# Indices of all edge blocks loaded once into SBUF, and the gather loop of a graph kernel written out

## The chip, the core and the metric

The kernel runs on one core of one Trainium2 chip. The metric is device time in microseconds of one execution, the median of several runs. The engines by their names in the rows: PE is the tensor engine, DVE the vector engine, ACT the scalar engine, POOL is GpSimd, SP the engine that here only issues DMAs. SPq and ACTq stand for the queues of DMAs issued by these engines.

## The reference

A graph attention network with two layers over 6250 nodes and 106,250 edges, and behind it a mixture of 8 experts. The edges are sorted by their destination.

```python
def _transformer_conv(x, edge_index, Wq, bq, Wk, bk, Wv, bv, Ws, bs):
    q = (x @ Wq.T + bq).reshape(N, H, C)          # H, C = 4, 16
    k = (x @ Wk.T + bk).reshape(N, H, C)
    v = (x @ Wv.T + bv).reshape(N, H, C)
    logits = (q[dst] * k[src]).sum(-1) * (1.0 / np.sqrt(C).astype(np.float32))
    m = jax.ops.segment_max(logits, dst, num_segments=N)
    e = jnp.exp(logits - m[dst])
    denom = jax.ops.segment_sum(e, dst, num_segments=N)
    alpha = e / (denom[dst] + 1e-16)
    msg = v[src] * alpha[..., None]
    out = jax.ops.segment_sum(msg, dst, num_segments=N).reshape(N, HC)
    return out + x @ Ws.T + bs
...
x = x + _L0_gnn_ref(_layernorm(x, axis=-1), edge_index, ...)
x = x + _L0_ffn_ref(_layernorm(x, axis=-1)[None], ...)[0]
```

The part that this document is about is `k[src]` and `v[src]`: for each edge, one row of keys and values is fetched by an index.

## The kernel before

There are five phases with a barrier of all engines between each two. The **setup** normalises the nodes, projects them to q, k, v and a skip path, stores a table of keys and values (`kv_t`, 512 bytes a node) in memory, finds for each node where its edges begin, fills a table with zeros (16 fills, L242) and scatters q to the places where a node's edges start (POOL, L126). The **edge phase** runs twice, once a layer (`edge_phase(0)`, `edge_phase(1)`), with a node phase between them that makes the tables of the second layer. The **expert phase** ends the kernel.

An edge phase works on 104 blocks (`BLOCKS`) of two streams of 512 edges, in 26 steps of four blocks (`UNROLL`). Each engine has its own program, and semaphores set the order:

- SP (L511 to L528) loads for block b, once the block four earlier has been transposed (`kq_turned`) and its logits used (`gaps_ready`): the indices `ix` (L518), the q rows `qz` (L519) and two masks (L521). Its DMAs stand in one queue in this order.
- POOL (L531 to L544) waits for the indices of the block and for its buffer (`v_turned`), and issues 8 gathers (L542) of 128 rows of keys and values each. `gathering` is a semaphore that it counts up and that no engine waits for.
- PE transposes k and q when the gathers have landed (L553, L554), multiplies for the logits (L560), transposes v (L566) and the results (L575 to L577), in four stages that lie one block apart.
- DVE runs the scans over the edges in three stages: held q (L603), the running maximum (L617) and differences (L622 to L625), the running sums (L631 to L638).
- ACT takes exponentials (L649) and stores the running sums (L657 to L664).

`each_step` (L483) writes out the first two steps of a phase (8 blocks) and puts the other 24 into a loop of the engine (`Fori`, L486), where the values waited for are in registers; `wait_past` is at L73, its wait at L76.

Of the kernel before, what the change touches and what calls it, by code (L numbers as in the profile page):

```python
# [20 lines left out]
I32 = mybir.dt.int32  # L21
# [5 lines left out]
P = 128  # L27
N, E, D = 6250, 106250, 256
HEADS, CH = 4, 16
HC = HEADS * CH  # L30
# [11 lines left out]
STREAMS = 2  # L42
STEP = 512
TPB = STEP // P
UNROLL = 4
# [45 lines left out]
def build(nc, d):  # L91
# [12 lines left out]
    with ExitStack() as whole:  # L104
        def keep(name, shape, dt=F32):
            return whole.enter_context(nc.sbuf_tensor(name, shape, dt))
# [11 lines left out]
        eps = keep("eps", [P, 1])  # L118
        skip = keep("skip", [P, NT, HC])

        proj = first.enter_context(nc.sbuf_tensor("proj", [P, NT, PROJ], F32))
# [38 lines left out]
        with ExitStack() as phase:  # L160
# [64 lines left out]
            def _(sp):  # L225
# [5 lines left out]
                sp.dma_start(b1[:, :], d["proj1_b"].partition_broadcast(P)).then_inc(w_in, 16)  # L231
                sp.dma_start(cut_ix[:, :], d["cut"]).then_inc(cut_in, 16)
                sp.wait_ge(zeroed, 1)

# [196 lines left out]
        def edge_sem(name):  # L431
            return whole.enter_context(nc.semaphore(name))

        ix_in = [edge_sem(f"ix_in{u}") for u in range(UNROLL)]
        kv_in = [edge_sem(f"kv_in{u}") for u in range(UNROLL)]
# [5 lines left out]
            "q_held", "kq_ready", "logits_ready", "carried", "top_ready"))  # L441
        grown, gaps_ready, ex_ready, weighted, v_summed, d_summed, copied, gathering = (edge_sem(n) for n in (
            "grown", "gaps_ready", "ex_ready", "weighted", "v_summed", "d_summed", "copied", "gathering"))

        w_in, w_high, w_parted = (edge_sem(n) for n in ("expert_w_in", "expert_w_high", "expert_w_parted"))

        def edge_phase(layer):
            with ExitStack() as phase:
# [6 lines left out]
                U = UNROLL  # L455
                ix = sb("ix", [P, U, TPB * STREAMS], I32)
                kv = sb("kv", [P, U, TPB, STREAMS * 2 * HC])
# [54 lines left out]
                def _(sp):  # L512
                    def body(i):
                        for u in range(U):
                            b = U * i + u
                            wait_past(sp, kq_turned, b - U + 1)
                            wait_past(sp, gaps_ready, b - U + 1)
                            sp.dma_start(ix[:, u, :], d["src"][b - BLOCKS * layer]).then_inc(ix_in[u], 16)  # L518
                            sp.dma_start(qz[:, u, :, :], qz_blocks[b - BLOCKS * layer]).then_inc(q_in[u], 16)  # L519
                            for s in range(STREAMS):  # L520
                                sp.dma_start(mask[HC * s:HC * (s + 1), u, :, :].rearrange("p m c -> p (m c)"),  # L521
                                             mask_t[s, b - BLOCKS * layer].partition_broadcast(HC)).then_inc(mask_in[u], 16)
# [8 lines left out]
                @block.gpsimd  # L531
                def _(pool):
                    def body(i):
                        for u in range(U):
                            b = U * i + u
                            pool.wait_ge(ix_in[u], 16 * i + 16)
                            wait_past(pool, v_turned, b - U + 1)
                            pool.sem_inc(gathering, 1)
                            for j in range(TPB):
                                for s in range(STREAMS):  # L540
                                    n = STREAMS * j + s
                                    pool.indirect_dma_start(kv[:, u, j, 2 * HC * s:2 * HC * (s + 1)], None, kv_t,  # L542
                                                            bass.IndirectOffsetOnAxis(ix[:, u, n:n + 1], 0)).then_inc(kv_in[u], 16)
                    each_step(pool, body)  # L544

# [912 lines left out]
```

## Time and profile before

| | us |
|---|---|
| median of 3 runs | 3950.41 |
| lowest, highest | 3943.72, 3952.69 |
| span of the profiled execution | 3586.4 |
| gathers of layer 0, first start to last end | 1087.9 |
| gathers of layer 1, first start to last end | 1092.3 |
| tensor engine busy | 2470.6 |
| vector engine busy | 2396.9 |
| GpSimd busy | 1938.3 |

The profile shows one execution. Its span reaches from the first to the last instruction; the device time of a run also holds what lies around that. Busy shares are over the whole span, though each phase has another engine at work: the 40 slices of the page show POOL at work from the start to slice 29, and PE near full from there on. The groups of instructions give for each its count, its busy time and mean, and the idle time of its engine ahead of it with the event that ended most of it; "issue" is a gap in which the engine waited for nothing that the profile shows.

### The profile page before, as it was taken

The page shows a single profiled execution, that of the slowest core. Times are in us where ns is not written, and L with a number is a line of the kernel's source. Part 1 is how long each engine was busy: PE and PEld are TensorE (multiplying, and loading weights), DVE is VectorE, ACT ScalarE, POOL GpSimd, SP SyncE. Part 2 cuts the span into 40 slices and gives each one's busy share as a digit, 9 for nine tenths or more (in the row PEclk, how much of TensorE's full clock was granted, in tenths as well). Part 3 has the DMA queues.
Part 4 walks back from the last instruction along what each step waited for, and adds up shares of the span by engine and source line. Part 5 has one row for each costly group of instructions (what it writes and reads, how often), then busy time and mean ns, then how long its engine had stood idle before and what let it go on. Part 6 is the DMA issues. An engine that isn't in the chain of part 4 may idle for free. (4 is left out here: it accounts for less than half of the span.)

```text
span 3586.4 us, 47557 instructions
## 1 busy us (share of the span) xinstructions
PE 2470.6 (69%) x13243; PEld 2120.5 (59%) x13243; DVE 2396.9 (67%) x3615; ACT 1117.9 (31%) x2130; POOL 1938.3 (54%) x1958
## 2 busy tenths in 40 slices
PE   1536666666566655266656566666589999999999
PEld 1425555555455544255545454555479989989998
DVE  3347777777777864387777777877655656556565
ACT  6301111111111111011111111111156656666666
POOL 6567777777777747677777777777410000000000
PEclk9756666666666655566666656666589999999999
DMA  9334444444454423344445454544300000000000
GB/s 377 129 96 134 123 132 131 126 131 124 127 129 128 129 66 81 88 137 138 128 128 138 129 137 131 142 133 135 91 17 11 13 25 11 13 24 1 21 11 11
DMA packets 394170, 356.45 MB, mean 99 GB/s; under 512 B 88694, under 2 KB 327436, under 8 KB 394080
## 3 DMA queue, kind: packets, MB, share of 16 engines
q1 hardware_dynamic: 221360, 168.40, 15.6%
q0 software_dynamic: 62896, 125.63, 14.4%
q10 hardware_dynamic: 109824, 61.36, 5.6%
q8 instruction: 40, 0.66, 0.1%
q14 instruction: 50, 0.41, 0.0%
HBM read 246.90 MB, written 108.30 MB: 99 GB/s over the span
## 5 line engine op out<-in xcount | busy, mean ns | idle before, releaser
L542 POOL DMA_INDIRECT kv<-kv_table,ix x1664 | 1673.5, 1006 | 530.9 <-issue 493.4
L553 PE MATMUL kT<-identity,kv 128*128 128x128 f32 x832 | 360.1, 434 | 916.8 <-DMA kv<-kv_table,ix 916.8
L649 ACT ACTIVATE ex<-gap 128x1024 f32<-128x1024 f32 x208 | 219.8, 1057 | 1742.1 <-DVE gap L625 1741.8
L553 PEld LDWEIGHTS kT<-identity,kv 128*128 128x128 f32 x832 | 182.6, 219 | 940.0 <-DMA kv<-kv_table,ix 686.6
L603 DVE TENSOR_TENSOR_SCAN held_q<-mask,held_q,qT 128x512 f32<-128x512 bf16 x208 | 265.9, 1278 | 485.9 <-PE qT L554 484.8
L1323 DVE TENSOR_TENSOR hid_lo_x<-full_x,hid_hi_x 128x448 fp32r<-128x448 f32 x448 | 276.0, 622 | 261.3 <-ACT hid_hi_x L1209 254.7
L1209 ACT ACTIVATE full_x<-psH_x,offset_x,scale_x 128x448 f32<-128x448 f32 x448 | 331.6, 740 | 285.2 <-PE psH_x L1064 285.1
L560 PE MATMUL logit<-kq,head_sum 128*128 128x512 f32 x416 | 389.9, 1040 | 2.6 <-DVE gap L625 2.6
L1013 POOL DMA_DIRECT2D x_x<-in_x x7 | 6.8, 971 | 631.4 <-DVE total_x L1367 631.4
L554 PE MATMUL qT<-identity,qz 128*128 128x128 f32 x832 | 346.5, 417 | 0.0
L577 PE MATMUL restT<-pick,top 128*128 128x8 f32 x1664 | 337.5, 275 | 0.0
L1209 ACT ACTIVATE hid_hi_x<-psH_x,offset_x,scale_x 128x448 fp32r<-128x448 f32 x448 | 331.7, 740 | 0.0
L576 PEld LDWEIGHTS restT<-pick,run_d 128*128 128x128 f32 x1664 | 322.0, 238 | 0.0
L566 PEld LDWEIGHTS vT<-identity,kv 128*128 128x128 f32 x832 | 172.5, 223 | 231.4 <-issue 228.4
L577 PEld LDWEIGHTS restT<-pick,top 128*128 128x128 f32 x1664 | 290.7, 219 | 0.0
L575 PE MATMUL outT<-identity,run_v 128*128 128x128 f32 x832 | 279.5, 336 | 4.7 <-DVE run_v L638 2.8
L576 PE MATMUL restT<-pick,run_d 128*128 128x8 f32 x1664 | 266.0, 232 | 0.0
L634 DVE TENSOR_TENSOR_SCAN run_d<-ex,run_d 128x512 f32<-128x512 f32 x208 | 264.8, 1273 | 0.0
L617 DVE TENSOR_TENSOR_SCAN top<-mask,top,logit 128x512 f32<-128x512 bf16 x208 | 264.0, 1269 | 0.0
L638 DVE TENSOR_TENSOR_SCAN run_v<-ex,run_v,wv 128x512 f32<-128x512 f32 x208 | 261.4, 1257 | 0.0
L1062 PE MATMUL psO_x<-expert_w_hi,hid_hi_x 128*128 128x256 f32 x784 | 223.3, 285 | 11.6 <-DVE hid_lo_x L1323 11.6
L1367 DVE SCALAR_TENSOR_TENSOR total_x<-psO_x,gate_x,total_x 128x256 f32<-128x256 f32 x343 | 161.5, 481 | 100.3 <-PE psO_x L1064 96.9
(209 smaller groups left out, 5240.1 us busy)
## 6 DMA issues: line engine op xcount, KB each, us to landing
running_sums<-rows ACTq DMA_DIRECT2D x208, 288.0 KB, 4.5
qz<-q_at_starts SPq DMA_DIRECT2D x208, 256.0 KB, 3.2
mask<-masks SPq DMA_DIRECT2D x416, 128.0 KB, 3.8
q_at_starts<-zeros SPq DMA_DIRECT2D x16, 1664.0 KB, 18.7
kv<-kv_table,ix POOLq DMA_INDIRECT x1664
x_sb<-in_x SPq DMA_DIRECT2D x1, 6272.0 KB, 27.6
kv_table<-proj SPq DMA_DIRECT2D x14, 448.0 KB, 3.2
x_x<-in_x POOLq DMA_DIRECT2D x7, 896.0 KB, 5.8
```

Of the source, the lines that this page charges most:

```text
L542: pool.indirect_dma_start(kv[:, u, j, 2 * HC * s:2 * HC * (s + 1)], None, kv_t, bass.IndirectOffsetOnAxis(ix[:, u, n:n + 1], 0)).then_inc( ...
L553: pe.transpose(kT[u % 2][:, P * j:P * (j + 1)], kv[:, u, j, 0::2], identity[:, :])
L554: ins = pe.transpose(qT[u % 2][:, P * j:P * (j + 1)], qz[:, u, j, :], identity[:, :])
L560: pe.matmul(logit[:, :], head_sum[:, :], kq[:, u % 2, :], start=True, stop=True)\
L575: pe.transpose(outT[:, of], run_v[:, u, of], identity[:, :])
L576: pe.matmul(restT[:, 0, j, :], run_d[:, u, of], pick[:, :], start=True, stop=True)
L577: ins = pe.matmul(restT[:, 1, j, :], top[:, u, 1 + P * j:1 + P * (j + 1)], pick[:, :], start=True, stop=True)
L603: dve.tensor_tensor_scan(held_q[:, h, :], mask[:, u, 0, :], qT[h][:, :], held_q[:, 1 - h, STEP - 1:STEP], ALU.mult, ALU.add).then_inc(q_he ...
L617: dve.tensor_tensor_scan(now, mask[:, u, 1, :], logit[:, :], last, ALU.add, ALU.max).then_inc(top_ready, 1)
L634: dve.tensor_tensor_scan(run_d[:, u, :], ex[:, h, 1, :], ex[:, h, 0, :], run_d[:, (u - 1) % U, STEP - 1:STEP], ALU.mult, ALU.add).then_inc ...
L1209: act.activation(to, psH[n % len(psH)][:, 0:HTOK], ACT.Relu, bias=offset[:, layer, at:at + 1], scale=scale[:, layer, at:at + 1]).then_inc( ...
L1323: dve.tensor_tensor(hid_lo[layer][:, m, of], full[:, n % 4, :], hid_hi[layer][:, m, of].bitcast(F32), ALU.subtract).then_inc(parted, 1)
```

## The change

The indices of all blocks get one buffer, `ix`, of 128 partitions by 104 x 8 numbers, kept for the whole kernel, and one DMA in the setup fills it, in SP's queue behind the cut indices. The host lays the array out to suit. The load per block (L518), its four semaphores and the small buffers go. POOL's loop is written out for all 104 blocks of a layer: one wait for the indices ahead of all, per block a wait for the buffer against a constant, and the 8 gathers. The semaphore `gathering` goes.

```diff
--- before.py
+++ after.py
@@ -117,6 +117,8 @@
         cut_q = keep("cut_q", [16, HC])
         eps = keep("eps", [P, 1])
         skip = keep("skip", [P, NT, HC])
+        ix = keep("ix", [P, BLOCKS, TPB * STREAMS], I32)
+        ix_in = whole.enter_context(nc.semaphore("ix_in"))
 
         proj = first.enter_context(nc.sbuf_tensor("proj", [P, NT, PROJ], F32))
 
@@ -230,6 +232,7 @@
                 sp.dma_start(w1t[:, :, :], d["proj1_w"].rearrange("(k p) c -> p k c", p=P)).then_inc(w_in, 16)
                 sp.dma_start(b1[:, :], d["proj1_b"].partition_broadcast(P)).then_inc(w_in, 16)
                 sp.dma_start(cut_ix[:, :], d["cut"]).then_inc(cut_in, 16)
+                sp.dma_start(ix[:, :, :], d["src"]).then_inc(ix_in, 16)
                 sp.wait_ge(zeroed, 1)
 
                 for m in range(FILLS):
@@ -431,7 +434,6 @@
         def edge_sem(name):
             return whole.enter_context(nc.semaphore(name))
 
-        ix_in = [edge_sem(f"ix_in{u}") for u in range(UNROLL)]
         kv_in = [edge_sem(f"kv_in{u}") for u in range(UNROLL)]
         q_in = [edge_sem(f"q_in{u}") for u in range(UNROLL)]
         mask_in = [edge_sem(f"mask_in{u}") for u in range(UNROLL)]
@@ -439,8 +441,8 @@
         cleared, kq_turned, v_turned, out_turned = (edge_sem(n) for n in ("cleared", "kq_turned", "v_turned", "out_turned"))
         q_held, kq_ready, logits_ready, carried, top_ready = (edge_sem(n) for n in (
             "q_held", "kq_ready", "logits_ready", "carried", "top_ready"))
-        grown, gaps_ready, ex_ready, weighted, v_summed, d_summed, copied, gathering = (edge_sem(n) for n in (
-            "grown", "gaps_ready", "ex_ready", "weighted", "v_summed", "d_summed", "copied", "gathering"))
+        grown, gaps_ready, ex_ready, weighted, v_summed, d_summed, copied = (edge_sem(n) for n in (
+            "grown", "gaps_ready", "ex_ready", "weighted", "v_summed", "d_summed", "copied"))
 
         w_in, w_high, w_parted = (edge_sem(n) for n in ("expert_w_in", "expert_w_high", "expert_w_parted"))
 
@@ -453,7 +455,6 @@
                     return phase.enter_context(nc.psum_tensor(f"{name}_{layer}", [P, STEP], F32))
 
                 U = UNROLL
-                ix = sb("ix", [P, U, TPB * STREAMS], I32)
                 kv = sb("kv", [P, U, TPB, STREAMS * 2 * HC])
                 qz = sb("qz", [P, U, TPB, STREAMS * HC])
                 mask = sb("mask", [P, U, 2, STEP], BF16)
@@ -515,7 +516,6 @@
                             b = U * i + u
                             wait_past(sp, kq_turned, b - U + 1)
                             wait_past(sp, gaps_ready, b - U + 1)
-                            sp.dma_start(ix[:, u, :], d["src"][b - BLOCKS * layer]).then_inc(ix_in[u], 16)
                             sp.dma_start(qz[:, u, :, :], qz_blocks[b - BLOCKS * layer]).then_inc(q_in[u], 16)
                             for s in range(STREAMS):
                                 sp.dma_start(mask[HC * s:HC * (s + 1), u, :, :].rearrange("p m c -> p (m c)"),
@@ -530,18 +530,15 @@
 
                 @block.gpsimd
                 def _(pool):
-                    def body(i):
-                        for u in range(U):
-                            b = U * i + u
-                            pool.wait_ge(ix_in[u], 16 * i + 16)
-                            wait_past(pool, v_turned, b - U + 1)
-                            pool.sem_inc(gathering, 1)
-                            for j in range(TPB):
-                                for s in range(STREAMS):
-                                    n = STREAMS * j + s
-                                    pool.indirect_dma_start(kv[:, u, j, 2 * HC * s:2 * HC * (s + 1)], None, kv_t,
-                                                            bass.IndirectOffsetOnAxis(ix[:, u, n:n + 1], 0)).then_inc(kv_in[u], 16)
-                    each_step(pool, body)
+                    pool.wait_ge(ix_in, 16)
+                    for b in range(BLOCKS):
+                        u = b % U
+                        wait_past(pool, v_turned, BLOCKS * layer + b - U + 1)
+                        for j in range(TPB):
+                            for s in range(STREAMS):
+                                n = STREAMS * j + s
+                                pool.indirect_dma_start(kv[:, u, j, 2 * HC * s:2 * HC * (s + 1)], None, kv_t,
+                                                        bass.IndirectOffsetOnAxis(ix[:, b, n:n + 1], 0)).then_inc(kv_in[u], 16)
 
                 @block.tensor
                 def _(pe):
@@ -1428,7 +1425,7 @@
     arrays = {
         "x": x,
 
-        "src": np.ascontiguousarray(src.reshape(STREAMS, BLOCKS, TPB, P).transpose(1, 3, 2, 0).reshape(BLOCKS, P, TPB * STREAMS)),
+        "src": np.ascontiguousarray(src.reshape(STREAMS, BLOCKS, TPB, P).transpose(3, 1, 2, 0).reshape(P, BLOCKS, TPB * STREAMS)),
         "dst": dst,
         "prev": np.concatenate([np.full(1, -1, np.int32), dst[:-1]]),
         "samples": np.ascontiguousarray(dst[:SROWS * SCOLS:SCOLS]),
```

On POOL, at the start of the first edge phase and in its loop, the order before is this (ix and kv are the index and gather buffers; the rows from 89 on are the loop):

```order
L542 DMA kv_0<-kv_table,ix_0 128x128 [waits ix_in2]
L542 DMA kv_0<-kv_table,ix_0 128x128 x7
L542 DMA kv_0<-kv_table,ix_0 128x128 [waits ix_in3]
L542 DMA kv_0<-kv_table,ix_0 128x128 x7
L542 DMA kv_0<-kv_table,ix_0 128x128 [waits ix_in0,v_turned]
L542 DMA kv_0<-kv_table,ix_0 128x128 x7
...
L486 ISA
L76 ISA [waits ix_in0]
L542 DMA kv_0<-kv_table,ix_0 128x128 [waits v_turned]
L542 DMA kv_0<-kv_table,ix_0 128x128 x7
L76 REGISTER_ALU [waits ix_in1]
```

The same place of POOL in the changed kernel, from the first gather on:

```order
L540 DMA kv_0<-kv_table,ix 128x128 [waits ix_in]
L540 DMA kv_0<-kv_table,ix 128x128 x31
L540 DMA kv_0<-kv_table,ix 128x128 [waits v_turned]
L540 DMA kv_0<-kv_table,ix 128x128 x7
L540 DMA kv_0<-kv_table,ix 128x128 [waits v_turned]
```

What moved: the waits for `ix_in0` to `ix_in3` and the register instructions between the blocks are gone, and POOL's program has 534 rows instead of 186.

On SP, a block inside the loop of the edge phase, before:

```order
L518 ISA [waits gaps_ready,kq_turned]
L518 DMA ix<-in_src 128x8
L519 ISA
L519 DMA qz<-q_at_starts 128x4x128
L521 REGISTER_ALU
L521 DMA mask<-masks 64x1024
```

and in the changed kernel, with the place in the setup where the one load now stands ahead of it:

```order
L235 DMA ix<-in_src 128x832
L245 DMA q_at_starts<-zeros 128x2x1664 [waits zeroed]
...
L519 ISA [waits gaps_ready,kq_turned]
L519 DMA qz_0<-q_at_starts 128x4x128
L521 ISA
L521 DMA mask_0<-masks 64x1024
```

What moved: in the loop, q is the first DMA behind SP's waits; in the setup, one DMA stands ahead of all fills.

## Rows read from the trace of the kernel before

**Rows 1.** The page: busy us by engine, and POOL's 40 slices in tenths.

```profile
PE 2470.6 (69%) x13243; PEld 2120.5 (59%) x13243; DVE 2396.9 (67%) x3615; ACT 1117.9 (31%) x2130; POOL 1938.3 (54%) x1958
...
POOL 6567777777777747677777777777410000000000
```

**Rows 2.** The page's groups: line engine op xcount | busy, mean ns | idle before, releaser.

```profile
L542 POOL DMA_INDIRECT kv<-kv_table,ix x1664 | 1673.5, 1006 | 530.9 <-issue 493.4
L553 PE MATMUL kT<-identity,kv 128*128 128x128 f32 x832 | 360.1, 434 | 916.8 <-DMA kv<-kv_table,ix 916.8
```

**Rows 3.** POOL's waits: total us, times, longest us.

```profile
POOL kv L542 <- issue: 493.4, 1619, 0.3
...
POOL kv L542 <- DMA ix<-in_src: 25.0, 4, 12.2
```

**Rows 4.** The two layers' rows of gathers: sum of length, POOL busy.

```profile
sum 2180.20, POOL 1673.46; mean POOL 836.73
```

**Rows 5.** Timeline of POOL (start, us, what) at the loop's entry and first jump.

```profile
279.39 1.32 POOL L542 DMA_INDIRECT kv<-kv_table,ix  x1 [0.30 <-issue]
...
321.48 0.95 POOL L542 DMA_INDIRECT kv<-kv_table,ix  x1 [0.30 <-issue]
```

**Rows 6.** Timeline behind the barriers of both edge phases and of the expert phase.

```profile
195.00 0.36 SPq L518 DMA_DIRECT2D ix<-in_src  x1
197.43 1.02 POOL L542 DMA_INDIRECT kv<-kv_table,ix  x1 [12.14 <-DMA ix<-in_src]
...
1458.15 0.36 SPq L518 DMA_DIRECT2D ix<-in_src  x1
1460.59 1.01 POOL L542 DMA_INDIRECT kv<-kv_table,ix  x1 [12.20 <-DMA ix<-in_src]
...
2585.32 0.34 SPq L988 DMA_DIRECT2D bn_x<-in_bn  x1
2586.00 1.03 POOL L1007 DMA_INDIRECT fin_x<-running_sums,end_row  x1 [33.25 <-POOLq L448]
```

**Rows 7.** Timeline of SP and POOL in the setup.

```profile
26.50 61.88 SPq L242 DMA_DIRECT2D q_at_starts<-zeros  x14
...
119.23 1.02 POOL L126 DMA_INDIRECT q_at_starts<-proj,start_row  x1 [30.80 <-DVEq L417]
```

**Rows 8.** The tile q_at_starts in the setup: its DMAs to landing.

```profile
DMA to landing us min/median/max: 1.6/18.6/23.6
```

**Rows 9.** Timeline of SP in two neighbouring blocks.

```profile
910.47 0.35 SPq L518 DMA_DIRECT2D ix<-in_src  x1
911.01 0.37 SPq L519 DMA_DIRECT2D qz<-q_at_starts  x1
...
919.14 0.35 SPq L518 DMA_DIRECT2D ix<-in_src  x1
```

**Rows 10.** Timeline of POOL there: last gathers of two blocks, and one between.

```profile
908.91 0.95 POOL L542 DMA_INDIRECT kv<-kv_table,ix  x1 [0.30 <-issue]
...
911.43 1.35 POOL L542 DMA_INDIRECT kv<-kv_table,ix  x1 [0.30 <-issue]
...
919.37 0.95 POOL L542 DMA_INDIRECT kv<-kv_table,ix  x1 [0.30 <-issue]
```

**Rows 11.** Timeline of PE there: the first transposes of the two blocks.

```profile
911.58 0.49 PE L553 MATMUL kT<-identity,kv 128*128 128x128 f32 x1 [2.56 <-DMA kv<-kv_table,ix]
...
923.09 0.48 PE L553 MATMUL kT<-identity,kv 128*128 128x128 f32 x1 [4.66 <-DMA kv<-kv_table,ix]
```

**Rows 12.** Timeline of DVE there.

```profile
911.94 1.25 DVE L638 TENSOR_TENSOR_SCAN run_v<-ex,run_v,wv 128x512 f32<-128x512 f32 x1
```

**Rows 13.** Stretches of 120 us, L542 alone (x gathers): emptiest and fullest of 18.

```profile
800.00:920.00 120.00, 92.99 (x89) 0.67 0.46 124
...
1465.00:1585.00 120.00, 91.31 (x95) 0.63 0.44 121
```

**Rows 14.** The page's larger instruction queue: packets, MB, share of 16 engines.

```profile
q8 instruction: 40, 0.66, 0.1%
```

## The prediction

> **What bounds the kernel now.** I began with the page's busy times and slices: no engine is above 69% of the span, and the GpSimd row (POOL) reads 7 in nearly every slice of the two edge phases and 0 in the expert phase behind them [rows 1]. The costliest group is the gather of the key and value rows, 1664 times 1006 ns; the tensor engine sits idle for 916.8 us ahead of the first transposes of the blocks, all of it put down to exactly these gathers [rows 2]. Then GpSimd's own waits: 1619 of the 1664 gathers begin after a gap put down to "issue", 0.3 us at the longest; 4 are put down to the indices, 25.0 us in all, of which 24.3 are the first gather of each phase [rows 3, 6]. The 41 that remain have 530.9 - 493.4 - 25.0 = 12.5 us, 0.3 us each, so they are the same gap under another name. GpSimd goes from gather to gather without a longer stop for 2180 of the 3586.4 us [rows 4], and the edge phases last as long as its issues do.
>
> What is outside this change: the expert phase, bound by the tensor engine, and what lies around the span, 3950.4 - 3586.4 = 364.0 us against the median. I keep both as they are and make the sum against the median.
>
> **Steady state, the waits and the loop.** Per block GpSimd loses the wait for the indices, a register instruction, and a semaphore increment that nobody waits for; per four blocks a loop branch. The first 64 gathers of a layer are written out already, the rest sit in the loop, so the trace holds both forms. The 65th gather, the first of the loop, starts at 279.39 after a gap of 0.30 us; the loop first branches back ahead of the 97th, at 321.48, after one of 0.30 us too: as between any two gathers inside a block [rows 5]. The removed instructions thus lie beside the gather in work. I cost them at nothing. What hides them is the 0.95 us of the gather ahead; with that cover gone they would cost a part of a 0.3 us gap, at 208 blocks 62 us at the very most.
>
> **The start of the two phases.** Today SP's first issue behind the barrier is the index load and GpSimd's first gather starts 197.43 - 195.00 = 2.43 us and 1460.59 - 1458.15 = 2.44 us later. Behind the barrier of the last phase, where the first gather of final rows waits for nothing of SP's, it starts 2586.00 - 2585.32 = 0.68 us after SP [rows 6]. The gain is 1.75 + 1.76 = 3.5 us; all of it is on the path, since everything in the phase follows the row of gathers. Its ends: 0 (something else late by as much) and 4.9 us. Most of the 12 us ahead of these gathers is not touched: the barrier itself ends only at 195.0.
>
> **The setup.** One load of 128 rows of 3328 bytes, 416 KB, is put into SP's queue behind the cut indices and ahead of the 16 fills of the q table, the two mask stores and the table stores. Behind the first two fills and the masks, fourteen fills of 1664 KB take SP 61.88 us, 4.4 us each; 416 KB is a quarter, 1.1 us, by which all of these move. Their last reader is GpSimd's scatter, which starts at 119.23 when the vector engine's row numbers are ready; the last fill is issued by 88.4 and lands 23.6 us later at the worst, at 112.0 [rows 7, 8]. There are 7.2 us of cover. Cost nothing; 1.1 us, were the cover gone.
>
> **The queue of SP in the loop.** This is the term that can be seen least. Per block SP issued the indices, then q, then two masks; q started 911.01 - 910.47 = 0.54 us behind the indices [rows 9]. Now q and the masks go out 0.54 us earlier, 208 times. Nobody waits for them as such, but they share the DMA engines with the last gather of a block. In two neighbouring blocks: the last gather of one ends at 909.86, ahead of SP's series, and the transposes start at 911.58, 1.72 us later [rows 9 to 11]; that of the next ends at 920.32, 1.18 us after SP's first issue of 919.14, and the transposes start only at 923.09, 2.77 us later. The vector engine's work follows the transposes, and here is why that matters although GpSimd waits for none of it: a gather takes 0.95 us, but longer when it meets the vector engine's sums. The gather of 911.43 took 1.35 us and ended at 912.78, 0.84 us into the scan of 911.94 (L638) [rows 10, 12]; that of 279.39 took 1.32 us [rows 5]. Over both layers this lengthening is 1673.5 - 1664 x 0.95 = 93 us [rows 2], and it hangs on how the vector engine's series falls against the grid of the gathers. Moving SP's series by 0.54 us deals this anew.
>
> Its size, from 18 stretches of 120 us: between 89 and 95 gathers are made in one, 11 of them have 92 or 93 [rows 13]. A gather on an edge is counted in both stretches, so I use only the ratio to their mean of 92.3. Were all like the best, the two rows of gathers would take 2180 x 92.3 / 95 = 2118 us, 62 less; like the worst, 2261, 81 more. These are the ends. The counts scatter by 1.5, a share of 1.6%, over 18 stretches 0.4%, that is 8 us; since today's sum is one such draw and the new one another, 11 us. The three times of the kernel before lie 9 us apart, which fits. As to the sign: the earlier series puts more last gathers behind it, which makes the transposes later and less even. I lean to +4 us, a twentieth of the 93; that is a judgement near zero, where most stretches lie, not a derivation.
>
> **Sum.** 3950.4 - 3.5 (starts) + 0 (loop and waits) + 0 (setup) + 4 (collisions) = 3951 us.
>
> **Rivals.**
> 1. Slower by collisions: the series from SP, 0.54 us earlier, meets the end of more blocks, the vector engine's scans shift onto the gathers. For it speaks that the two blocks above lie 1.8 us apart in this respect and stand on the two sides of the edge; against it, that the stretches already hold all cases and average out. If the mean fell by 1%, from 92.3 to 91.4 gathers in 120 us, it would cost 22 us: 3950.4 - 3.5 + 22 = 3969. It decides from half of that, 11 us: 3958, 0.2% above the time before.
> 2. Faster by the same means: a mean higher by 1%, 93.2 gathers, gives 3950.4 - 3.5 - 22 = 3925; by half of that 3936.
> 3. The written-out stream stalls: a layer has 832 gathers in its program instead of 96. The larger instruction queue moved 0.66 MB in 40 packets during the whole run, 16 KB each [rows 14]; if the added 1472 gathers brought some ten such fetches, each in the open for a microsecond or two, it would be 3951 + 15 = 3966. Against it: the 64 gathers written out keep the 0.30 us gap.
> 4. The branch did cost: each of some 46 jumps back stalls GpSimd for a microsecond, and the change gives 46 us back: 3905. The gap ahead of 321.48 says no.
> 5. The change does not reach the path at all (the start is held by something else): 3954 and within 0.2%, counted with the forecast.
>
> The Trainium skill (Runtime: NRT & Kernel Launch, Instruction fetch mechanics) says that a taken branch to a target outside the pages held forces a fetch before execution goes on, and that kernels therefore prefer full unrolling; by it rival 4 would be the forecast. The trace does not agree here: the gap at the loop's jump is that between any two gathers [rows 5]. The same section says straight code is fetched ahead, which speaks against rival 3.
>
> **Chances and range.** 0.2% of the time is 7.9 us, about what a measurement of this kernel can tell from no change. Forecast with rival 5: 52%. Rival 1: 25%, rival 3: 5%, together slower 30%. Rival 2: 16%, rival 4: 2%, together faster 18%. The scatter of 11 us, and some for the median, gives 8 in 10 within 15 us; I widen upwards for rivals 1 and 3: 3936 to 3968.
>
> **What would show it.** The first gathers of both phases start 0.7 us after SP's first issue, with no wait for indices. The gap between gathers stays 0.30 us everywhere; if it falls, the loop was paid for and I am wrong in the main. GpSimd's L540 group has 1664 instructions of 0.995 to 1.02 us on average; every 0.01 us is 17 us, so this mean alone says which rival holds. A gap of over 0.5 us between gathers not put down to a buffer is rival 3. The scatter of the setup still starts at 119 to 120 us. In a block, SP's issue of q stands where that of the indices stood, directly ahead of the masks.

## The result, and the profile after

The change made the kernel faster: 3882.24 us, median of 4 runs (3876.62 to 3884.49), against 3947.06 for the kernel before in the same comparison (4 runs, 3939.33 to 3952.69). The ratio is 0.9834, 95% interval 0.9815 to 0.9852. The prediction said 3951, 3936 to 3968, and gave "faster" 18%.

The experiments later met a chip on which the kernel before takes 3600 to 3607 us. The comparisons therefore come from two kinds of chip, told apart by the kernel before alone: three chips, and the comparison above, where it takes 3944 to 3972 us (called A here), and one (B). What is said below holds for the kind named. The profiled execution shown for the kernel before, with its span of 3586.4 us, is by that span of kind B; the three times beside it are of kind A.

The page of the kernel after, kind A: span, 40 slices of POOL, and three groups of instructions (line engine op xcount | busy, mean ns | idle before, releaser).

```profile
span 3878.5 us, 46469 instructions
...
POOL 6466766776767747566666776766720000000000
...
L540 POOL DMA_INDIRECT kv<-kv_table,ix x1664 | 1688.7, 1015 | 748.8 <-issue 478.3
...
L600 DVE TENSOR_TENSOR_SCAN held_q<-mask,held_q,qT 128x512 f32<-128x512 bf16 x208 | 263.7, 1268 | 735.0 <-remote 690.4
...
L654 ACT ACTIVATE rows<-outT 128x512 f32<-128x512 f32 x208 | 122.2, 587 | 705.0 <-remote 681.8
```

The span lies 1.7 us under the time of that run, 3880.24. The gathers have 1015 ns each; they had 1006 in [rows 2]. But the idle time ahead of them is 748.8 us, where [rows 2] show 530.9, and two groups wait for something "remote" (a semaphore moved, and the profile finds no instruction that had just ended to tie it to), which isn't among the waits of [rows 3]. POOL's waits in the kernel after:

```profile
POOL kv L540 <- issue: 478.3, 1557, 0.9
POOL kv L540 <- remote: 249.6, 105, 5.4
```

So the two profiles at hand, before and after, couldn't be compared: against [rows 4] the edge phases of the faster kernel are 236 us longer. The first thing needed was a profile of the kernel before that belongs to its time.

### The profile page after: what moved, and what is told of

Same layout as the page of the kernel before. It is cut to its first block and busy times, and to the rows that moved or that the text cites. A ratio compares the mean times of both kernels' runs of the same rounds, so it can differ in the third digit from the quotient of the medians.

```text
span 3878.5 us, 46469 instructions
## 1 busy us (share of the span) xinstructions
PE 2641.4 (68%) x13243; PEld 2233.3 (58%) x13243; DVE 2388.1 (62%) x3615; ACT 1128.4 (29%) x2130; POOL 1955.0 (50%) x1958
## 5 line engine op out<-in xcount | busy, mean ns | idle before, releaser
L540 POOL DMA_INDIRECT kv<-kv_table,ix x1664 | 1688.7, 1015 | 748.8 <-issue 478.3
L572 PE MATMUL outT<-identity,run_v 128*128 128x128 f32 x832 | 329.5, 396 | 544.8 <-ACT rows L657 490.0
L550 PE MATMUL kT<-identity,kv 128*128 128x128 f32 x832 | 344.6, 419 | 337.9 <-DMA kv<-kv_table,ix 299.1
L572 PEld LDWEIGHTS outT<-identity,run_v 128*128 128x128 f32 x832 | 228.2, 274 | 590.9 <-ACT rows L657 493.1
L574 PE MATMUL restT<-pick,top 128*128 128x8 f32 x1664 | 402.6, 315 | 1.8 <-issue 1.8
L573 PEld LDWEIGHTS restT<-pick,run_d 128*128 128x128 f32 x1664 | 401.9, 293 | 0.0
L574 PEld LDWEIGHTS restT<-pick,top 128*128 128x128 f32 x1664 | 366.4, 271 | 0.0
L551 PE MATMUL qT<-identity,qz 128*128 128x128 f32 x832 | 333.4, 404 | 0.3 <-issue 0.3
L654 ACT ACTIVATE rows<-outT 128x512 f32<-128x512 f32 x208 | 122.2, 587 | 705.0 <-remote 681.8
L573 PE MATMUL restT<-pick,run_d 128*128 128x8 f32 x1664 | 310.0, 259 | 0.0
```

The costliest lines, as they stand in the source:

```text
L550: pe.transpose(kT[u % 2][:, P * j:P * (j + 1)], kv[:, u, j, 0::2], identity[:, :])
L551: ins = pe.transpose(qT[u % 2][:, P * j:P * (j + 1)], qz[:, u, j, :], identity[:, :])
L572: pe.transpose(outT[:, of], run_v[:, u, of], identity[:, :])
L573: pe.matmul(restT[:, 0, j, :], run_d[:, u, of], pick[:, :], start=True, stop=True)
L574: ins = pe.matmul(restT[:, 1, j, :], top[:, u, 1 + P * j:1 + P * (j + 1)], pick[:, :], start=True, stop=True)
```

## The kernel before, profiled again

> The kernel before, unchanged, profiled once more. Its rows read ahead of the prediction show GpSimd issuing a gather every 1.25 to 1.31 us and a span of 3586 us against a device time of 3950 us, while the changed kernel's span is 3878.5 us with a time of 3880.2 us. Theory A (the earlier profiled execution was not like the timed ones): span within 3 us of its own time, so about 3945 us, and GpSimd waits for buffers as in the changed kernel, over 250 us in all. Theory B (364 us really lie around the span in the kernel before and the change removes them): span about 3586 us again, rows of gathers 1088 and 1092 us.

It took 3941.45 us, with a span of 3939.7. Its page, the same parts, and POOL's waits:

```profile
span 3939.7 us, 47557 instructions
...
POOL 5456767677666755566676676666641000000000
...
L542 POOL DMA_INDIRECT kv<-kv_table,ix x1664 | 1716.4, 1031 | 797.0 <-issue 583.3
...
L603 DVE TENSOR_TENSOR_SCAN held_q<-mask,held_q,qT 128x512 f32<-128x512 bf16 x208 | 263.9, 1269 | 767.9 <-remote 624.6
```

```profile
POOL kv L542 <- issue: 583.3, 1594, 6.3
POOL kv L542 <- remote: 183.5, 61, 4.2
```

Nothing like 364 us lies around the span; it is 1.75 us. The wait put down to "issue" is 6.3 us at its longest, where [rows 3] have 0.3. GpSimd does not go from gather to gather here: it makes 107 stops of more than 0.35 us between gathers (counted in its timeline), 98 of them ahead of the first gather of a block, 267 us in all beyond the usual 0.30.

The two rows of gathers, from the first start to the last end of each layer, POOL's gathers alone (us, busy, count, clock, DMA share, GB/s), before and then after, kind A:

```profile
211.81:1460.21 1248.40, 867.71 (x832) 0.61 0.41 111
1657.24:2897.74 1240.50, 848.65 (x832) 0.60 0.43 117
```

```profile
211.19:1417.94 1206.75, 846.32 (x832) 0.61 0.41 115
1616.07:2825.88 1209.81, 842.34 (x832) 0.63 0.42 119
```

The sum falls from 2488.9 to 2416.6 us, by 72 (the times by 61 to 65; these are single executions). Of it 1716.4 - 1688.7 = 28 us are shorter gathers and 44 fewer or shorter stops. This is where the time went: into the rows of gathers. Why the gathers themselves got shorter was not found.

## Which part of the change it is

Four kernels of one comparison ran on one chip, kind A, with the kernel before at 3944.58 us.

> The changed kernel, unchanged, as the yardstick of this series: time 3875 to 3890 us, 0.983 of the kernel before, span 2 us below its time, GpSimd waits for buffers of some 250 us. Both theories expect the same.

Measured: 3878.80 us, ratio 0.9836 (0.981 to 0.9862). The gain repeats.

**The loop written out, alone.** The kernel before, its index load and wait per block kept (the semaphore `gathering` goes too):

```diff
-                    def body(i):
-                        for u in range(U):
-                            b = U * i + u
-                            pool.wait_ge(ix_in[u], 16 * i + 16)
+                    for n_b in range(BLOCKS):
+                        b = BLOCKS * layer + n_b
+                        u = b % U
+                        pool.wait_ge(ix_in[u], 16 * (b // U) + 16)
```

> The loop written out with constant waits, but the indices still loaded block by block through SP's queue. Theory 1 (the gain of 65 us comes from taking 208 index loads and their 0.54 us each out of SP's series and off the DMA engines): about 3947 us, as before. Theory 2 (the loop and its register waits held GpSimd): about 3882 us, as the changed kernel.

Measured: 3939.33 us, ratio 0.9989 (0.997 to 1.0008). The form of the loop is worth nothing, in either direction: it neither pays for branches nor stalls the stream of instructions.

**The loads, put back without their use.** The kernel after, with a load of the block's indices into a buffer that nobody reads or waits for:

```diff
+                            sp.dma_start(ix_again[:, u, :], src_blocks[b - BLOCKS * layer]).then_inc(again_in[u], 16)
                             sp.dma_start(qz[:, u, :, :], qz_blocks[b - BLOCKS * layer]).then_inc(q_in[u], 16)
```

> The changed kernel with the 208 index loads of 4 KB put back into SP's series ahead of q, into a buffer that nobody reads or waits for. Theory 1 (SP's queue): the gain is lost, about 3947 us. Theory 2 (the loop): about 3882 us.

Measured: 3884.33 us, ratio 0.9852 (0.9825 to 0.988). The 208 loads in SP's queue cost a few us at most. What is left is GpSimd's wait for them.

**The wait put back.** The next four ran on another chip of kind A, before at 3947.13. To the kernel with the unread loads, one line on GpSimd, which still reads the resident indices:

```diff
                         u = b % U
+                        pool.wait_ge(again_in[u], 16 * ((BLOCKS * layer + b) // U) + 16)
                         wait_past(pool, v_turned, BLOCKS * layer + b - U + 1)
```

> The kernel after the change, with the 208 index loads put back on SP's queue into buffers of their own (as in the run with the unread loads), and now GpSimd also waits, with a constant, for the load of a block before it gathers the block. Its gathers still read the resident indices, so only the dependence is put back. Theory A (the gain is the dependence: the index load of block b can be issued only once block b-4 has been turned and its gaps are made, and lands a few us later, and the gathers started behind it): the time of the kernel before comes back, ratio 0.996 to 1.000, some 3935 to 3945 us, and the long gaps between gathers sum to about 265 us again. Rival B (the gain is in how the gathers read their indices, from a buffer that nothing writes): it stays at the time of the kernel after, ratio 0.983 to 0.986, some 3880 to 3885 us.

Measured: 3934.82 us, ratio 0.9972 (0.9959 to 0.9986). One wait per block brings back 1.2 of the 1.5%. Its gathers on the page:

```profile
L545 POOL DMA_INDIRECT kv<-kv_table,ix x1664 | 1710.8, 1028 | 796.1 <-issue 487.7
```

1028 ns and 796.1 us are the 1031 and 797.0 of the kernel before. That it is this wait is shown; how it costs is read below, and the last 0.3% isn't accounted for.

**The load early, the wait kept.** The kernel before with a ring of 8 index buffers, the load issued four blocks sooner, SP's and GpSimd's series written out (the two lines that move the load):

```diff
+                            if b + U < U * (past + STEPS):
+                                load_ix(b + U)
-                            sp.dma_start(ix[:, u, :], d["src"][b - BLOCKS * layer]).then_inc(ix_in[u], 16)
```

> The kernel before with its index load per block kept, and kept as a wait of GpSimd's, but into a ring of 8 buffers and issued four blocks earlier, in the place of SP's series where the load of block b stood now stands that of block b+4; the first four stand at the head of the phase. For that, SP's series and GpSimd's are written out with constant waits. Theory A (a load that lands late): the load is 40 us early now, and the time is that of the kernel after, ratio 0.982 to 0.987, some 3876 to 3890 us, without any resident indices. Rival B (the gain is in a resident buffer that nothing writes while it is read): ratio 0.996 to 1.001, some 3935 to 3950 us.

Measured: 3921.96 us, ratio 0.9919 (0.9892 to 0.9946), between the two expectations. A load issued some 40 us ahead would hardly land late, and yet half of the loss stays while GpSimd waits for it. Either such a wait costs something even when it is long met, or SP's written-out series costs the rest. For the second, SP's series alone written out in the kernel after:

> The kernel after the change, with SP's series of loads (qz and the two masks of each block) written out with constant waits, in the same order, and nothing else changed. It asks why the kernel with the index loads four blocks ahead won back only 0.8% of the 1.65%: there SP's series had to be written out too, and SP then spaces its issues 0.4 to 0.5 us apart and not 1.4 to 2.2. Theory F (the form of SP's series costs, its faster issues meeting the gathers): this comes out at 3905 to 3925 us, ratio 0.990 to 0.994. Rival G (the form is worth nothing, and what is left lies in the wait for a load of its own): 3872 to 3888 us, ratio 0.982 to 0.986.

It met the chip of kind B (before 3606.76) and gave 3604.88, ratio 1.0018 (0.9997 to 1.004). That says nothing on kind A; the next section finds the first in the trace, and enough of it that nothing has to be left for the second.

## What the stops are

The plain reading of the wait that was put back is: the index load comes late. The trace of the kernel before on kind A speaks against it. SP's issues, and GpSimd's last gathers of one block and the first of the next (start, us, what, [idle before <- releaser]):

```profile
916.73 0.07 SPq L518 DMA_DIRECT2D ix<-in_src  x1
918.88 0.70 SPq L519 DMA_DIRECT2D qz<-q_at_starts  x1
921.12 1.43 SPq L521 DMA_DIRECT2D mask<-masks  x2
```

```profile
926.63 0.95 POOL L542 DMA_INDIRECT kv<-kv_table,ix  x1 [0.30 <-issue]
930.49 1.11 POOL L542 DMA_INDIRECT kv<-kv_table,ix  x1 [2.91 <-remote]
```

```profile
922.60 1.06 PE L566 MATMUL vT<-identity,kv 128*128 128x128 f32 x4
```

The block that starts at 930.49 had its indices issued at 916.73, 13.8 us earlier (on kind B the first load of a phase is met by its gather in 2.4 us [rows 6]), and the value transposes that free its kv buffer ran at 922.60. GpSimd stood for 2.91 us with both behind it. Lined up by block number, of 48 such stops in layer 0 none has its index load issued less than 9.4 us before, nor the transposes started less than 3.8.

Other engines stand in the same way, and come off together. The kernel after on kind A (the second profile of it), all engines around 929.8, and the transposes and SP's mask issue of the block whose scan starts there:

```profile
929.63 0.60 ACT L654 ACTIVATE rows<-outT 128x512 f32<-128x512 f32 x1 [8.77 <-remote]
929.81 1.28 DVE L600 TENSOR_TENSOR_SCAN held_q<-mask,held_q,qT 128x512 f32<-128x512 bf16 x1 [7.07 <-remote]
929.98 0.95 POOL L540 DMA_INDIRECT kv<-kv_table,ix  x1 [2.65 <-remote]
```

```profile
918.85 0.48 PE L550 MATMUL kT<-identity,kv 128*128 128x128 f32 x1 [1.56 <-DMA kv<-kv_table,ix]
...
920.40 0.42 PE L551 MATMUL qT<-identity,qz 128*128 128x128 f32 x1
```

```profile
899.79 2.20 SPq L521 DMA_DIRECT2D mask<-masks  x2
```

VectorE's scan needs the transposes (done by 920.82) and the masks (issued at 899.79), and VectorE was free at 922.74; it starts at 929.81. ScalarE and GpSimd, which wait for other semaphores, start within 0.35 us of it. The same three start within 0.45 us of each other 26 times in that layer. By block number, the scan starts after the block's first transpose in a median of 8.6 us here and 5.4 in the kernel before on kind A, but 2.02 on kind B, where nine blocks in ten lie between 2.01 and 2.18.

**Whose signals are late.** The trace also keeps the times at which the semaphores moved, and they name the late ones. What the three engines waited for around 929.8 are three signals of one engine: the results turned (out_turned, moved at 929.53), keys and queries turned (kq_turned, 929.62) and values turned (v_turned, 929.72). All three are TensorE's, whose instructions for them had ended at 917.28, 920.82 and 922.98. In the two layers of the first profile of the kernel after, all the "remote" waits of the rows above, 97 of VectorE, 90 of ScalarE and 105 of GpSimd, end with these three semaphores. In that stretch a signal of VectorE or ScalarE that ends a wait moves its semaphore at most 13 ns after the instruction; TensorE's do so in a median of 8.3 us, against 14 ns in the profile of the kernel before on kind B. So on kind A TensorE's signals arrive late, or its work is really done later than the profile, which models the ends of matmuls, puts it; the record can't tell these two apart, nor say what causes either. The DMA packets are as long on both kinds (a mean of 0.265 us for a 4096-byte packet of the gathers, before, on B and on A).

**How the removed wait costs.** It isn't the wait that ends last. In the kernel before the program's wait for this block's indices is passed at 918.10, 12.4 us ahead of the gather at 930.49; the stop ends with v_turned, at 929.70, as do 95 of the 98 ahead of a block. But two waits ahead of one gather give the sequencer, the part of GpSimd that takes its instructions in order, an instruction more. GpSimd's wait instructions of the helper at L76, first with the index wait put back and then in the kernel after (its second profile; xcount, then ns):

```profile
L76 POOLq EVENT_SEMAPHORE  x204: 17/17/1799, 257.8 to 2879.0; - x102
```

```profile
L76 POOLq EVENT_SEMAPHORE  x1: 17/17/17, 1615.8 to 1615.8; - x1
```

```profile
POOL kv L545 <- remote: 281.6, 93, 6.2
```

With one wait, the gather itself waits for v_turned and starts 0.258 us after the semaphore moves (105 stops of the first profile of the kernel after, 0.257 to 0.259). With both, v_turned has an instruction of its own, and the gather starts a median of 0.760 us after the signal where the index wait was put back (93 stops), 0.759 with the loop alone written out, 0.760 with the load early, and 0.794 in the kernel before. While GpSimd has a gather in work this hides behind it: kind B has the same instructions and keeps its gaps of 0.30 us. Where GpSimd stands, it is in the open. An estimate from these rows: 0.50 us in 93 stops are 47 us, where putting the wait back cost 48; with the load early, 80 stops are 40 us, where that kernel lies some 38 above 0.984 of its comparison's time. The longer gathers of the kernels with the wait (1028 to 1031 ns against 1015) are not part of this, and stay unexplained.

## Attempts at what is left

On kind A, in the comparison with before at 3947.13:

> The kernel after the change, with the two mask loads of a block put ahead of its qz load in SP's series. It asks what bounds the kernel now: in the trace of after, VectorE's first scan of a block waits for the mask's landing (about 690 us in 97 waits). If the late mask sets the pace of the blocks (theory C), the masks come some 2 us sooner and up to 2 us in about half of the 208 blocks is saved: 3.0 to 5 per cent of nothing hidden, at most 200 us, and I expect 10 to 60 us less, 3820 to 3870. If the gathers set it and the mask wait only fills VectorE's idle time (theory D), it is within 0.3% of after: 3870 to 3890.

The edit puts the `qz` issue behind the loop over the two masks. Measured: 3872.87 us, ratio 0.9807 (0.9791 to 0.9824), 0.3% below the change's; the two intervals overlap, so this isn't settled. Theory C's 10 to 60 us are there at their lower end or not at all. Its premise falls with the semaphores: the 690 us in 97 waits end with kq_turned, not with a mask. It is the lowest time on kind A.

> The kernel with the index loads four blocks ahead, and with four buffers instead of two for the rows that ScalarE stores (four semaphores for them). In the traces of before and after ScalarE waits 458 and 682 us for the store of two blocks before. If that wait holds the blocks up (theory E), it goes, and the time falls against the same kernel with two buffers by 10 to 60 us, to 3820 to 3870. If the gathers set the pace (theory D), it is within 0.3% of the one with two buffers, 3870 to 3890.

Measured: 3919.54 us, ratio 0.9928 (0.9908 to 0.9948), that of the same kernel with two buffers, 0.9919; both absolute ranges, 3820 to 3870 and 3870 to 3890, were missed, since the kernel it builds on takes 3921.96. ScalarE's wait isn't for its store: the 458 and 682 us end with out_turned, and such waits are 641 us with two buffers and 613 with four.

The next edit aims at the release of the kv buffers; TensorE's stage for the values of an earlier block goes to the front of its series (the stage list's loop changes to suit):

```diff
-                    each_block(pe, [turn_kq, logits, turn_v, turn_results])
+                    each_block(pe, [turn_kq, logits, turn_v, turn_results], first=2)
```

> The kernel after the change, with TensorE's turning of the values of block b-2 put first in its series for block b, ahead of the wait for block b's gathers; the three other stages follow in their order. It asks what bounds the kernel after the change. Theory D (GpSimd's long gaps, 221 us in all, are waits for the release of a kv buffer, which comes from that turning): the release comes some us earlier, most of the long gaps go, and the time falls by 60 to 200 us, to 3680 to 3820 us. Rival H (the gaps come from further back, from VectorE's chain that the turning waits for in any order): within 0.5% of after, 3862 to 3895 us.

> Both edits to the kernel after the change: the mask loads ahead of the qz load, and the turning of the values first in TensorE's series. The first alone gave 3872.9 against about 3883. By theory D it falls by the same 60 to 200 us as the turning alone, and some 0 to 10 us further; by rival H it stays at 3855 to 3885 us.

> The kernel before, index loads and waits as they were, with the turning of the values first in TensorE's series. Theory A with D (in the kernel before, a block's gathers wait for its index load, which is released by the block's own gaps and not by the turning; an earlier release of kv buffers then meets that wait): it gains little, within 0.5% of before or at most 1%, 3905 to 3950 us, while the same edit gains 60 us or more after the change. Rival I (buffer release alone sets the pace in both): it falls by as much as the edit on the kernel after does.

These were the first on the chip of kind B, before at 3606.76: 3580.85 (0.9936, 0.9913 to 0.9958), 3574.87 (0.9917, 0.989 to 0.9944) and 3567.67 (0.9899, 0.9855 to 0.9943). On B there are no stops to win back, so the expectations can't be judged. In the last, shorter gathers are most of it: 986 ns against the 1006 of [rows 2], 33 us over 1664, of 39.

**The kernel after on kind B.** The same chip again, before at 3600.06.

> The kernel after the change, unchanged. In the last comparison the kernel before itself took 3607 us, against 3947 us in the three earlier ones, and its profile had no long gap between gathers in it, like the profiled execution that the prediction was made from. So there are two conditions of the chip, told apart by the kernel before alone. Theory J (the gain belongs to the condition with long gaps): where the kernel before takes about 3605 us, the change is worth nothing or costs a little, ratio 0.997 to 1.004; where it takes about 3945 us, the ratio is 0.984 again. Rival K (the gain is there in both): ratio 0.982 to 0.988 at 3605 us too.

Measured: 3595.68 us in 12 runs, ratio 0.9992 (0.9968 to 1.0016). Theory J holds: on kind B the change does nothing that can be measured. Its page, its waits, and the starts of the first phase:

```profile
span 3593.3 us, 46469 instructions
...
L540 POOL DMA_INDIRECT kv<-kv_table,ix x1664 | 1678.1, 1008 | 527.4 <-issue 506.4
...
L600 DVE TENSOR_TENSOR_SCAN held_q<-mask,held_q,qT 128x512 f32<-128x512 bf16 x208 | 265.9, 1278 | 487.6 <-PE qT L551 487.2
```

```profile
POOL kv L540 <- issue: 506.4, 1662, 0.3
```

```profile
194.49 0.39 SPq L519 DMA_DIRECT2D qz<-q_at_starts  x1
```

```profile
195.20 1.02 POOL L540 DMA_INDIRECT kv<-kv_table,ix  x1 [10.45 <-POOLq L162]
```

No gap over 0.3 us behind the first gather of a phase, and VectorE waits for TensorE by name, not for something remote.

> The change with the turning of the values first in TensorE's series, once more. Where the kernel before takes about 3945 us, this is its first comparison there. Theory D (GpSimd's long gaps are waits for a kv buffer's release): it takes 60 to 200 us off the kernel after, ratio to before 0.93 to 0.97. Rival L (the engines that stand there have all they need already, by the trace, and an earlier release changes nothing): 0.980 to 0.986. Where the kernel before takes about 3605 us, both expect the 0.9936 of the first comparison again.

> The kernel before with the turning of the values first, once more. At about 3605 us it should give 0.990 again. At about 3945 us theory A (its gathers wait for their index load, which an earlier release of kv buffers doesn't hasten) expects 0.995 to 1.000, and rival I (buffer release alone sets the pace) 0.93 to 0.98.

Kind B again: 3576.50 (0.9925, 0.9901 to 0.9949) and 3565.65 (0.9914, 0.9881 to 0.9947), as before. The profile of the first has gathers of 1008 ns, so shorter gathers aren't needed for this gain; it is the longest of its runs, 3592.35.

The last comparison met a third chip of kind A, before at 3971.59:

> The change with the turning of the values first in TensorE's series, a third time, for a comparison where the kernel before takes about 3945 us. Theory D (release of kv buffers): ratio 0.93 to 0.97 there. Rival L (the engines that stand have all they need): 0.980 to 0.986 there. Where the kernel before takes about 3600 us: 0.993 again, which tells neither apart.

> The kernel before with the same edit, a third time. Where the kernel before takes about 3945 us: theory A 0.995 to 1.000, rival I 0.93 to 0.98. Where it takes about 3600 us: 0.990 to 0.992 again.

Measured: 3927.26 us, ratio 0.9881 (0.9852 to 0.991), and 4061.09, ratio 1.0221 (1.0188 to 1.0253). Theory D falls, and rival I with it: an earlier release of the buffers brings none of the 60 to 200 us on kind A. Rival L's 0.980 to 0.986 is missed too, though the interval reaches into it; the kernel after the change wasn't run on this chip, so that a part of its gain is given back is likely, not shown. The kernel before gets 2.2% slower. The waits of the first of the two show a price:

```profile
PE vT L563 <- DVE wv L628: 660.7, 157, 26.0
```

With the values' transposes first in its series, TensorE now stands behind VectorE's reading of the last values, and by the order of its program the next block's key transposes wait with it. Against theory A, which expected 0.995 to 1.000 there, the second is a miss too. In its profile GpSimd's stops are 458 us against the 267 of the kernel before on another chip of kind A, and its gathers 94 us shorter (1621.9 against 1716.4), together 97 us, near the 89.5 between the times; here the index load does come last in 19 waits, 129.2 us in all, where it was 3 and 28.3. On kind B the same edit wins nearly 1%: what pays there can't be carried to A.

## Why the prediction was wrong

**What lies around the span, 364.0 us, "kept as is".** The term that failed in the sum is "loop and waits, 0", below; this step is why it looked safe. The 364 themselves cancel in the sum, which starts from 3950.4. The difference of 10% between the profiled execution and the times was booked as a constant, though no row showed any of it, and every wait was then read in an execution that lacked it. On every chip met, a run lies 1.7 to 1.8 us above its own span. Of the 353 us between the two spans of the kernel before, 2488.9 - 2180.2 = 309 are in the rows of gathers [rows 4]. The Trainium skill (Runtime: NRT & Kernel Launch, The ~15µs preamble/postamble breakdown) puts some 15 us around a kernel; the runs here show less still, and either number would have refused 364.

**What bounds the kernel.** "Issue-bound, 0.30 us between gathers everywhere" is right on kind B, before and after, and wrong on kind A, where the stops sum to 267 us before and 222 after (second profile of it). Everything weighed in the prediction, its five rivals included, was a mechanism of the profile shown. "Nobody waits for them", of q and the masks, is wrong as the program goes, since TensorE waits for the one and VectorE for the others; but in the profile it was read from no wait is put down to either.

**Starts, -3.5 us.** On kind B GpSimd's first gather comes 195.20 - 194.49 = 0.71 us after SP's first issue, as said; the two layers' rows are 1084.56 and 1099.98 us, together 4.3 more than in [rows 4].

**Loop and waits, 0.** The loop: right, 0.9989 on kind A. There the wait for the indices was most of the case, and this is the term that failed: "they lie beside the gather in work", costed at nothing. It costs some 48 us in 208 blocks, the difference of 3934.82 and 3884.33 less the 2.5 by which the chips differ, because in 90 to 100 of them no gather is in work when v_turned comes, and the second wait then delays the gather by 0.50 us. The prediction named this case ("with that cover gone") and its bound, 62 us at the most, held, but took it for absent; its price, "a part of a 0.3 us gap", was too low per block. On kind B it costs nothing.

**Setup, 0.** Right: the scatter starts at 119.72 us in the kernel after, 119.23 in [rows 7].

**Collisions, +4.** On kind B the gathers went from 1673.5 to 1678.1 us, 4.6 more, but 1690.4 in the kernel with SP written out: the sign can't be told from single profiles. On kind A they fell by 28 us, where +4 was forecast: 1031 and 1028 ns with the wait, 1015 without. So this term was mis-sized too. That it is a shift of VectorE's series that deals them anew was not tested.

**Rivals.** Rival 4, the loop's branches at 3905, stood nearest to the time; that is luck, for the loop written out alone refutes it as a mechanism. The Trainium skill (Runtime: NRT & Kernel Launch, Instruction fetch mechanics) asks for full unrolling because of the jumps; here 46 jumps of GpSimd are worth 0.11% with an interval that holds zero. Rival 3 is refuted by the same run, on kind A. On kind B, forecast and range of the change (+0.5 us of 3600, ratio 1.000) hold: 0.9992.

## What to carry to other kernels

Before any row of a profile is read, set its span against the times: if they are more than a few us apart, the profile belongs to another kernel or another condition of the chip, and must be taken again before anything is priced from it. A second wait ahead of an instruction can cost though it is met long before: it takes the first wait off the instruction, which here then started 0.50 us later after the signal. It is hidden while the engine is busy and paid where it stands, so removing it gained on one kind of chip and nothing on the other (0.9834 and 0.9992). An edit that chains engines more tightly can win 1% on one chip and lose 2% on the next. When engines that wait for different things start together, ask whose signals they all are. Measure on more than one chip, each time beside the kernel before.

## What was not expected of the hardware

- The same kernel takes 3600 to 3607 us on one chip and 3944 to 3972 on three others, 9 to 10% more, with DMA packets of equal length and a granted clock of 0.74 against 0.71. All of the profiled executions on the three show "remote" waits of VectorE of 16 to 26 us at the longest, those on the other none. Whether this belongs to the chip or to something around it wasn't settled.
- On those three, of the engines' signals that end a wait TensorE's are late, by a median of 4.0 to 8.3 us in each profile, while VectorE's and ScalarE's come within 14 ns. Engines that wait for different signals of TensorE start within 0.45 us of each other.
- The profiles on those three hold only 21 to 26% of the semaphore increments that their DMAs must have made, and some 76% of the engines'; those on the other chip 99 to 100%. Every time on record comes with a span, so no run tells whether those chips are as slow without a profiler at work. That is a rival for the whole of kind A, and untested.
- A gather that waits itself starts 0.258 us after the semaphore moves; behind a wait instruction of its own, 0.76 to 0.79 us.
- 1664 gathers written out instead of in a loop over 32: no difference (0.9989, 0.997 to 1.0008).
- A DMA issued and not waited for, 208 times in SP's queue: 3878.80 to 3884.33 us, 5.5 us by the medians, with ratio intervals that overlap.
